# One beat less of lag in the gate pipeline of a transformer block, and its last copies shared by two engines

## The chip, the cores and the metric

The kernel runs on one core of a Trainium2 chip. The metric is the device time of one execution in microseconds (us). TensorE multiplies and transposes, ScalarE and VectorE work element by element, GpSimd does the same for work off their hands, and SyncE issues DMAs. Each engine runs its own queue in order; engines meet by semaphores only.

## The reference

The reference is a transformer block on x of 4 x 32 x 32 x 192: attention with decomposed relative positions (12 heads of 16), then a mixture of 8 experts in which each of the 4096 tokens takes its best one. The change touches what lies between the two:

```python
x = x + _L0_conv_ref(_ln_c(x), ...)          # ends with: out @ proj_w.T + proj_b
t = _to_tokens(x)
t = t + _L0_ffn_ref(_ln_t(t), ...)           # begins with: gate = xf @ Wg.T + bg
...
def _ln_t(v, eps=1e-05):
    m = jnp.mean(v, axis=-1, keepdims=True)
    s = jnp.var(v, axis=-1, keepdims=True)
    return (v - m) / jnp.sqrt(s + eps)
```

## The kernel before

Five functions run one after the other, with all engines meeting between them: `project`, `attention`, `gate` (L960), `route` (L1274) and `experts` (L1386). The change is in `gate` alone. It handles the 4096 tokens in 8 steps of 512 tokens (`STEPS`), each of 4 tiles of 128 tokens (`TPS`). What a step s goes through, with the short names that this document uses:

- **T(s), A(s)**: `turn_attention` (L1061) transposes the attention output on TensorE into `at_ps`; `copy_attention` (L1126) copies its two parts on ScalarE.
- **P(s)**: `project_out` (L1070), 16 float32 matmuls on TensorE. Its input is A(s).
- **R(s)**: `residual` (L1181) on VectorE, two additions into x_sb and four of statistics.
- **root**: `take_root` for the steps of `ROOTS`: (0, 1), (2, 3), (4, 5), (6) and (7), called roots 0 to 4. VectorE makes the variance in five small instructions (L1247 to L1253), ScalarE takes the square root (L1138), VectorE makes `rstd` and `shift` in five more (L1257 to L1265). In each engine's queue nothing passes it.
- **N(s)**: `normalize` (L1034) on GpSimd, four instructions (L1042), which need the root of the step. The last step's is on VectorE (L1219), after root 4.
- **H(s)**: `split_high` (L1148) on ScalarE, the float16 high part of the normalized rows (L1154).
- **L(s)**: `split_low` (L1192) on VectorE, the rest that H(s) leaves (L1195).
- **D(s)**: `double_tails` (L1045) on GpSimd (L1049); after it SyncE stores the step's parts to HBM (L1016), the residual having been stored at L1012.
- **U(s)**: `turn_normalized` (L1083) on TensorE, 8 transposes of the high half and 8 of the low half into two PSUM banks, one bank for each half (L1091).
- **C(s)**: `copy_normalized` (L1140) on ScalarE, the high and the low bank, 128x1024 float16 each (L1146).
- **G(s)**: `gates` (L1094) on TensorE, 16 small matmuls into `gate_ps`.

After G(7), VectorE adds the bias to the gate values (L1226, L1228), and the engines meet before `route` begins.

The order in each queue is written out by hand, as a loop over beats b. With `LAG = 3`, a beat of the kernel before is, for all b at which the step numbers are valid:

- TensorE: T(b+1), P(b), U(b-4), G(b-5)
- ScalarE: A(b+1), the square root of the root that ended at beat b-1, H(b-3), C(b-4)
- VectorE: L(b-4), R(b), the root that ends with step b; at b = 7 also L(4) and N(7); L(5) to L(7) after it
- GpSimd: D(b-4), N(b-2)
- SyncE: the residual's store of b, the parts' store of b-4

Waits that bear on the order: T(s) needs A(s-1); U(s) needs D(s) and both halves of C(s-1); G(s) needs C(s); C(s) needs U(s) and G(s-2); N(s) and H(s) need their slot of three free, that is L(s-3), and for H(s) also U(s-3) and the store of s-3.

Of the kernel before, what the change touches and what calls it, by code (L numbers as in the profile page):

```python
# [20 lines left out]
ALU = mybir.AluOpType  # L21
ACT = mybir.ActivationFunctionType
# [11 lines left out]
STEPS = T // HALF  # L34
TPS = HALF // P
# [924 lines left out]
def gate(nc, g):  # L960

    LAG = 3
    ROOTS = ((0, 2), (2, 4), (4, 6), (6, 7), (7, 8))
    BANKS, SLOTS = 3, 3
    CONSTS = 16 * (7 + len(ROUTE_TABLES))
# [2 lines left out]
    with ExitStack() as ctx:  # L968
        sb = lambda name, shape, dt=F32: ctx.enter_context(nc.sbuf_tensor(name, shape, dt))
        sem = lambda name: ctx.enter_context(nc.semaphore(name))  # L970
        w, wg = g.proj_w, g.gate_w
        at = [sb("at_top", [C, 2, HALF]), sb("at_bottom", [C + 1, 2, HALF])]
        tt = [sb("tt_hi", [P, 2, 2 * HALF], F16), sb("tt_lo", [P, 2, 2 * HALF], F16)]
# [17 lines left out]
        last_ready = sem("last_tn_ready")  # L991
        tn_hi_done, tn_lo_done, tails_doubled = sem("tn_hi_done"), sem("tn_lo_done"), sem("tails_doubled")
        x1_stored, tn_stored = sem("x1_stored"), [sem(f"tn_stored{j}") for j in range(SLOTS)]
        tt_ps_ready, tt_ready, gate_ready, gate_copied = sem("tt_ps_ready"), sem("tt_ready"), sem("gate_ready"), sem("gate_copied")
        gate_split = sem("gate_split")
        block = ctx.enter_context(nc.Block())

# [7 lines left out]
        @block.sync  # L1005
        def _(sp):
            load_experts(sp, g, experts_loaded)

            def store_residual(s):
                sp.wait_ge(x1_ready, 2 * s + 2)  # L1010
                tiles = slice(TPS * s, TPS * (s + 1))
                sp.dma_start(g.token_tiles[:, tiles, AT_X:ROW], g.x_sb[:, tiles, :]).then_inc(x1_stored, 16)  # L1012

            def store_normalized(s):
                sp.wait_ge(tails_doubled, s + 1)
                sp.dma_start(g.token_tiles[:, TPS * s:TPS * (s + 1), 0:AT_X],  # L1016
                             parts[:, s % SLOTS].rearrange("p t q d -> p t (q d)").bitcast(F32)).then_inc(tn_stored[s % SLOTS], 16)

            for b in range(STEPS + LAG + 1):
                if b < STEPS:  # L1020
                    store_residual(b)
                if b >= LAG + 1:
                    store_normalized(b - LAG - 1)
            sp.wait_ge(x1_stored, 16 * STEPS)
            for j in range(SLOTS):
                sp.wait_ge(tn_stored[j], 16 * len(range(j, STEPS, SLOTS)))
            sp.wait_ge(experts_loaded, 16 * (EXPERTS // 2))

        @block.gpsimd
        def _(pool):  # L1030
            nc.gpsimd.memset(g.slot_rows[:], 0.0).then_inc(rows_zeroed, 1)
            pool.wait_ge(rows_zeroed, 1)

            def normalize(s):  # L1034
                pool.wait_ge(shift_done, root_of(s) + 1)
                if s >= SLOTS:

                    pool.wait_ge(tn_hi_done, s - SLOTS + 1)
                    pool.wait_ge(tn_lo_done, s - SLOTS + 1)
                for i in range(TPS):  # L1040
                    t = TPS * s + i
                    last = nc.gpsimd.tensor_scalar(tn[:, s % SLOTS, i, :], g.x_sb[:, t, :], rstd[:, t:t + 1], shift[:, t:t + 1], ALU.mult, ALU.add)  # L1042
                last.then_inc(tn_ready, 1)

            def double_tails(s):  # L1045

                pool.wait_ge(tn_lo_done, s + 1)
                both = parts[:, s % SLOTS]
                nc.gpsimd.tensor_copy(both[:, :, :, D:ROW_PART], both[:, :, :, P:D]).then_inc(tails_doubled, 1)  # L1049

            for b in range(2, STEPS + LAG + 1):
                if b >= LAG + 1:
                    double_tails(b - LAG - 1)
                if b - 2 < STEPS - 1:
                    normalize(b - 2)

        @block.tensor
        def _(pe):
# [23 lines left out]

            def turn_normalized(s):  # L1083
                pe.wait_ge(tails_doubled, s + 1)
                if s:
                    pe.wait_ge(tt_ready, 2 * s)
                for part in range(2):
                    for i in range(TPS):
                        for c in range(2):
                            at = c * HALF + i * P  # L1090
                            last = nc.tensor.transpose(tt_ps[part][:, at:at + P], parts[:, s % SLOTS, i, part, c * P:(c + 1) * P], g.ident16[:])  # L1091
                    last.then_inc(tt_ps_ready, 1)

            def gates(s):  # L1094
                pe.wait_ge(tt_ready, 2 * s + 2)
                for i in range(TPS):
                    t = TPS * s + i
                    both, high = (g_ps[:, 2 * t * EXPERTS:(2 * t + n) * EXPERTS] for n in (2, 1))
                    (top_hi, tail_hi), (top_lo, tail_lo) = ([rows[:, s % 2, c * HALF + i * P:c * HALF + (i + 1) * P] for c in range(2)] for rows in tt)
                    nc.tensor.matmul(both, top_hi, w16[0][:], start=True, stop=False, skip_group_check=True)  # L1100
                    nc.tensor.matmul(high, top_lo, w16[0][:, 0:EXPERTS], start=False, stop=False, skip_group_check=True)
                    nc.tensor.matmul(high, tail_hi, w16[1][:, 0:EXPERTS], start=False, stop=False, skip_group_check=True)
                    last = nc.tensor.matmul(high, tail_lo, w16[1][:, EXPERTS:], start=False, stop=True, skip_group_check=True)
                last.then_inc(gate_ready, 1)

            turn_attention(0)
            pe.wait_ge(ones_set, 1)
            for b in range(STEPS + LAG + 2):
                if b + 1 < STEPS:
                    turn_attention(b + 1)  # L1110
                if b < STEPS:
                    project_out(b)
                if LAG + 1 <= b < STEPS + LAG + 1:
                    turn_normalized(b - LAG - 1)
                if b == LAG + 2:
                    pe.wait_ge(gate_split, 6)
                if b >= LAG + 2:
                    gates(b - LAG - 2)

        @block.scalar  # L1120
        def _(act):
# [15 lines left out]
                tiles = slice(TPS * first, TPS * last)  # L1137
                nc.scalar.activation(rstd[:, tiles], var[:, tiles], ACT.Sqrt).then_inc(root_done, 1)  # L1138

            def copy_normalized(s):  # L1140
                for c in range(2):
                    act.wait_ge(tt_ps_ready, 2 * s + c + 1)
                    if s >= 2 and c == 0:

                        act.wait_ge(gate_ready, s - 1)
                    nc.scalar.activation(tt[c][:, s % 2, :], tt_ps[c][:], ACT.Copy).then_inc(tt_ready, 1)  # L1146

            def split_high(s):  # L1148
                wait_normalized(act, s)
                if s >= SLOTS:  # L1150

                    act.wait_ge(tn_stored[s % SLOTS], 16 * (s // SLOTS))
                    act.wait_ge(tt_ps_ready, 2 * (s - SLOTS) + 2)
                nc.scalar.activation(parts[:, s % SLOTS, :, 0, 0:D], tn[:, s % SLOTS], ACT.Copy).then_inc(tn_hi_done, 1)  # L1154

            copy_attention(0)
            for b in range(STEPS + LAG + 1):
                if b + 1 < STEPS:
                    copy_attention(b + 1)
                if b - 1 in ended:  # L1160
                    take_root(ended[b - 1])
                if LAG <= b < STEPS + LAG:
                    split_high(b - LAG)
                if b >= LAG + 1:
                    copy_normalized(b - LAG - 1)

        @block.vector
        def _(dve):
# [23 lines left out]
            def split_low(s):  # L1192
                dve.wait_ge(tn_hi_done, s + 1)
                both = parts[:, s % SLOTS]
                nc.vector.tensor_tensor(both[:, :, 1, 0:D], tn[:, s % SLOTS], both[:, :, 0, 0:D], ALU.subtract).then_inc(tn_lo_done, 1)  # L1195
# [4 lines left out]
                inverse_root(nc, dve, stats, mean, var, rstd, shift, tmp, EPS_FFN, chain, root, root_done, shift_done,  # L1200
                             tiles=slice(TPS * first, TPS * last), calls=r)

            for b in range(STEPS + LAG + 1):
                if LAG + 1 <= b < STEPS:
                    split_low(b - LAG - 1)
                if b < STEPS:
                    residual(b)
                if b in ended:
                    take_root(ended[b])
                if b == STEPS - 1:  # L1210

                    split_low(b - LAG)
                    s = STEPS - 1
                    dve.wait_ge(shift_done, len(ROOTS))
                    dve.wait_ge(tn_hi_done, s - SLOTS + 1)
                    dve.wait_ge(tn_lo_done, s - SLOTS + 1)
                    for i in range(TPS):
                        t = TPS * s + i
                        nc.vector.tensor_scalar(tn[:, s % SLOTS, i, :], g.x_sb[:, t, :], rstd[:, t:t + 1], shift[:, t:t + 1],  # L1219
                                                ALU.mult, ALU.add).then_inc(last_ready, 1)  # L1220
                if b > STEPS:
                    split_low(b - LAG - 1)
# [485 lines left out]
```

## Time and profile before

| | us |
|---|---|
| median of 3 runs | 914.4 (911.68 to 914.62) |
| the profiled execution's own time | 910.65 |
| its span, first to last instruction | 908.8 |
| `project` | 0 to about 85 |
| `attention` | to about 672 |
| `gate` | about 672 to 731 |
| `route` | about 731 to 752 |
| `experts` | to the end |

Over the whole span TensorE is busy 89%, VectorE 80%, ScalarE 67% and GpSimd 30%. These shares say little on the change, since it lies in 59 of 909 us: in there, what counts is which wait ends last before each engine's next instruction. Times of the trace are counted from the start of the span.

### The profile page before, as it was taken

What the parts mean: (1) busy time and instruction counts of PE and PEld (TensorE: products, weight loads), DVE (VectorE), ACT (ScalarE), POOL (GpSimd) and SP (SyncE); (2) the same over time, 40 slices, a digit from 0 to 9 for tenths busy, and PEclk for the clock granted to TensorE, in tenths of its full rate; (3) what the DMA queues carried; (4) which work ended last, traced back from release to release, by engine and by line L of the source; (5) the groups of instructions that cost most, each with busy time, mean ns of one, the idle gap of its engine ahead of it and who ended that gap; (6) DMA issues with size and microseconds to landing.
All of it is one profiled execution on the core that took longest, in us unless ns stands there. A gap on an engine that the chain in (4) does not pass through costs nothing. (4 is left out here: it accounts for less than half of the span.)

```text
span 908.8 us, 26203 instructions
## 1 busy us (share of the span) xinstructions
PE 810.6 (89%) x8970; PEld 448.2 (49%) x8970; DVE 725.3 (80%) x1026; ACT 611.1 (67%) x1139; POOL 275.9 (30%) x431
## 2 busy tenths in 40 slices
PE   3889946999999999999999999999989526999994
PEld 1657931333333333333333333333348516999994
DVE  6756766898899989999999999989627676888883
ACT  3556623888888888888888888888865513444452
POOL 2460000013342343302223242431114404656552
PEclk9989975999999999999999999999999757999998
DMA  6234783344544444434444444553135402222320
GB/s 170 79 91 130 321 313 91 96 119 132 141 133 120 135 131 129 118 113 122 131 134 131 138 132 120 140 152 98 25 122 169 159 16 70 80 83 80 88 60 12
DMA packets 69733, 109.63 MB, mean 121 GB/s; under 512 B 20139, under 2 KB 36681, under 8 KB 68146
## 3 DMA queue, kind: packets, MB, share of 16 engines
q1 hardware_dynamic: 59120, 75.49, 28.6%
q0 software_dynamic: 9248, 26.51, 10.0%
q10 hardware_dynamic: 1314, 6.95, 2.0%
q8 instruction: 31, 0.51, 0.2%
q14 instruction: 20, 0.16, 0.1%
HBM read 77.58 MB, written 33.19 MB: 122 GB/s over the span
## 5 line engine op out<-in xcount | busy, mean ns | idle before, releaser
L907 DVE TENSOR_REDUCE neg_max<-max_ps 128x1 f16<-128x1024 f32 x384 | 452.2, 1222 | 54.4 <-PE max_ps L761 54.0
L890 ACT ACTIVATE probs<-ring_ps 128x512 f32<-128x512 f32 x768 | 413.6, 595 | 69.9 <-PE ring_ps L793 68.5
L793 PE MATMUL ring_ps<-q_side,k_side 113*128 113x512 f16 x768 | 234.6, 387 | 6.0 <-DMA q_side<-rel_split 4.0
L805 PE MATMUL out_ps<-probs,values 128*32 128x256 f32 x3072 | 206.4, 386 | 0.1
L761 PE MATMUL max_ps<-k_side,q_side 48*128 48x256 f16 x1536 | 123.0, 279 | 15.6 <-ACT ident L865 9.1
L805 PEld LDWEIGHTS out_ps<-probs,values 128*32 128x32 f32 x3072 | 80.3, 109 | 111.1 <-ACT probs L890 56.2
L657 POOL COPY max_copies<-neg_max 128x32 f16<-128x32 f16 x48 | 10.1, 211 | 365.7 <-DVE neg_max L907 365.7
L761 PEld LDWEIGHTS max_ps<-k_side,q_side 48*128 48x128 f16 x1536 | 50.2, 95 | 114.6 <-issue 66.4
L793 PEld LDWEIGHTS ring_ps<-q_side,k_side 113*128 113x128 f16 x768 | 51.8, 97 | 104.9 <-ACT probs L890 73.1
L1461 PE MATMUL hid_ps<-slot_t,w_top 128*118 128x128 f16 x312 | 69.6, 223 | 0.8 <-ACT slot_t L1507 0.8
L1462 PE MATMUL hid_ps<-slot_t,w_top 128*118 128x128 f16 x312 | 68.9, 221 | 0.0
L1463 PE MATMUL hid_ps<-slot_t,w_top 128*118 128x128 f16 x312 | 68.9, 221 | 0.0
L1464 PE MATMUL hid_ps<-slot_t,w_tail 128*118 128x128 f16 x312 | 68.9, 221 | 0.0
L1465 PE MATMUL hid_ps<-slot_t,w_tail 128*118 128x128 f16 x312 | 68.9, 221 | 0.0
L1517 ACT ACTIVATE silu<-hid_ps 118x512 f32<-118x512 f32 x39 | 23.3, 597 | 50.5 <-PE hid_ps L1465 50.5
L1440 POOL DMA_INDIRECT out<-y,slot_token x39 | 39.5, 1012 | 54.4 <-issue 36.8
L1425 POOL DMA_INDIRECT slot_rows<-token_rows,slot_token x39 | 42.2, 1082 | 39.1 <-SPq L1388 27.4
L1564 DVE TENSOR_TENSOR hidden<-hid_ps,silu 118x512 f32<-118x512 f32 x39 | 27.0, 691 | 27.2 <-ACT silu L1517 19.4
L1461 PEld LDWEIGHTS hid_ps<-slot_t,w_top 128*118 128x118 f16 x312 | 41.9, 134 | 4.0 <-issue 2.3
L1462 PEld LDWEIGHTS hid_ps<-slot_t,w_top 128*118 128x118 f16 x312 | 42.0, 135 | 0.0
L1463 PEld LDWEIGHTS hid_ps<-slot_t,w_top 128*118 128x118 f16 x312 | 42.0, 135 | 0.0
L1465 PEld LDWEIGHTS hid_ps<-slot_t,w_tail 128*118 128x118 f16 x312 | 42.0, 134 | 0.0
(228 smaller groups left out, 1321.0 us busy)
## 6 DMA issues: line engine op xcount, KB each, us to landing
q_side<-rel_split SPq DMA_DIRECT2D x384, 64.0 KB, 2.3
q_side<-qk_split SPq DMA_DIRECT2D x192, 64.0 KB, 2.5
rel_split<-expert_weights ACTq DMA_DIRECT2D x6, 1024.0 KB, 5.0
rel_split<-expert_weights SPq DMA_DIRECT2D x6, 1024.0 KB, 6.1
q_side<-qk_split SPq DMA_DIRECT2D x48, 128.0 KB, 2.7
k_side<-qk_split SPq DMA_DIRECT2D x144, 32.0 KB, 1.7
token_rows<-tn_parts SPq DMA_DIRECT2D x8, 512.0 KB, 3.5
expert_weights<-in_w_t POOLq DMA_DIRECT2D x32, 117.2 KB, 2.9
```

The costliest lines, as they stand in the source:

```text
L761: last = nc.tensor.matmul(max_ps[t % 2][:, keys], q_side[j][at:at + HIGH, quarter, t * P:(t + 1) * P], k_side[j][at:at + HIGH, keys], star ...
L793: nc.tensor.matmul(ring_ps[turn_of(k) % BANKS][:], k_side[slot(s)][:, tile * P:(tile + 1) * P], q_side[slot(s)][:, tile // 2, (i % 2) * HA ...
L805: last = nc.tensor.matmul(out_ps[quarter * 2 * HD:(quarter + 1) * 2 * HD, :], values[j][:, tile, :], probs[:, u % 2 * GROUP + 2 * i + quar ...
L890: nc.scalar.activation(probs[:, u % 2 * GROUP + i, :], ring_ps[turn_of(k) % BANKS][:], ACT.Exp).then_inc(exp_done, 1)
L907: nc.vector.tensor_reduce(neg_max[:, j % 2, t:t + 1], max_ps[t % 2][:], AX, ALU.max, negate=True).then_inc(tile_max, 1)
L1425: pool.indirect_dma_start(rows[:, j, :], None, g.token_rows, bass.IndirectOffsetOnAxis(ap=g.slot_token[:, n:n + 1], axis=0), bounds_check= ...
L1440: pool.indirect_dma_start(g.out_rows, bass.IndirectOffsetOnAxis(ap=g.slot_token[:, n:n + 1], axis=0), y[:, j, :], None, bounds_check=last_ ...
L1461: nc.tensor.matmul(out, w_top[:, j, h, 0, some], hi_top, start=True, stop=False, skip_group_check=True)
L1462: nc.tensor.matmul(out, w_top[:, j, h, 0, some], lo_top, start=False, stop=False, skip_group_check=True)
L1463: nc.tensor.matmul(out, w_top[:, j, h, 1, some], hi_top, start=False, stop=False, skip_group_check=True)
L1464: nc.tensor.matmul(out, w_tail[:, j, h, some], hi_tail, start=False, stop=False, skip_group_check=True)
L1465: last = nc.tensor.matmul(out, w_tail[:, j, h, some], lo_tail, start=False, stop=True, skip_group_check=True)
```

## The change

Every later member of a step's chain moves up by one beat, relative to T(b+1), P(b) and R(b), which stay. A beat is now:

- TensorE: T(b+1), P(b), U(b-3), G(b-4)
- ScalarE: A(b+1), the square root, H(b-2), C(b-3). After beat 7: root 4, H(6), high half of C(5), H(7), high half of C(6), high half of C(7)
- VectorE: L(b-3), R(b), the root. After beat 7: L(5), N(7), L(6), L(7), low halves of C(5), C(6), C(7)
- GpSimd: D(b-3), N(b-2); at b = 7 N(5) and N(6) both
- SyncE: the residual's store of b, the parts' store of b-3

The semaphore `tt_ready` becomes two, one for each half, so that U(s) can begin with the high half when the high bank is free. The number of instructions that compute is the same; three copies move from ScalarE to VectorE.

```diff
+    EARLY = STEPS - LAG
...
-            for b in range(2, STEPS + LAG + 1):
-                if b >= LAG + 1:
-                    double_tails(b - LAG - 1)
-                if b - 2 < STEPS - 1:
+            for b in range(2, STEPS + LAG):
+                if b >= LAG:
+                    double_tails(b - LAG)
+                if b < STEPS:
                     normalize(b - 2)
+                if b == STEPS - 1:
+                    normalize(STEPS - 2)
...
                 pe.wait_ge(tails_doubled, s + 1)
-                if s:
-                    pe.wait_ge(tt_ready, 2 * s)
                 for part in range(2):
+                    if s:
+                        pe.wait_ge(tt_ready[part], s)
...
-                if LAG + 1 <= b < STEPS + LAG + 1:
-                    turn_normalized(b - LAG - 1)
+                if LAG <= b < STEPS + LAG:
+                    turn_normalized(b - LAG)
...
             copy_attention(0)
-            for b in range(STEPS + LAG + 1):
+            for b in range(STEPS):
                 if b + 1 < STEPS:
                     copy_attention(b + 1)
                 if b - 1 in ended:
                     take_root(ended[b - 1])
-                if LAG <= b < STEPS + LAG:
-                    split_high(b - LAG)
-                if b >= LAG + 1:
-                    copy_normalized(b - LAG - 1)
+                if b >= 2:
+                    split_high(b - 2)
+                if b >= LAG:
+                    for c in range(2):
+                        copy_turned(b - LAG, c)
+            take_root(len(ROOTS) - 1)
+            split_high(STEPS - 2)
+            copy_turned(STEPS - 3, 0)
+            split_high(STEPS - 1)
+            copy_turned(STEPS - 2, 0)
+            copy_turned(STEPS - 1, 0)
...
+            def copy_low(s):
+                dve.wait_ge(tt_ps_ready, 2 * s + 2)
+                dve.wait_ge(gate_ready, s - 1)
+                nc.vector.tensor_copy(tt[1][:, s % 2, :], tt_ps[1][:]).then_inc(tt_ready[1], 1)
+
+            for b in range(STEPS):
+                if b >= LAG:
+                    split_low(b - LAG)
+                residual(b)
                 if b in ended:
                     take_root(ended[b])
...
+            for n in range(EARLY + 1, STEPS):
+                split_low(n)
+            for n in range(EARLY, STEPS):
+                copy_low(n)
```

## Rows read from the trace of the kernel before

**Rows 1.** Stretches: length, busy per engine (instructions), TensorE clock, DMA share, GB/s.
```profile
693.00:715.00 22.00, 15.40 (x179) 14.37 (x177) 16.81 (x62) 13.21 (x20) 10.89 (x20) 0.98 0.50 164
715.00:731.00 16.00, 9.72 (x144) 9.35 (x144) 6.38 (x11) 9.22 (x10) 5.24 (x8) 0.50 0.40 138
```

**Rows 2.** Waits of 672 to 731: who, for whom, us in total, times, longest.
```profile
POOL tn_parts L1049 <- DVE tn_parts L1195: 18.6, 6, 5.0
ACT tt_hi L1146 <- PE tt_hi_ps L1091: 14.0, 8, 3.0
DVE rstd L1257 <- ACT rstd L1138: 3.2, 5, 1.2
```

**Rows 3.** Timeline of VectorE, L(3) and L(4): start, duration, instruction, idle before.
```profile
708.84 0.18 DVE L1257 RECIPROCAL rstd<-rstd 128x4 f32<-128x4 f32 x1 [0.68 <-ACT rstd L1138]
...
709.72 0.95 DVE L1195 TENSOR_TENSOR tn_parts<-tn,tn_parts 128x768 f16<-128x768 f32 x1
...
715.07 0.95 DVE L1195 TENSOR_TENSOR tn_parts<-tn,tn_parts 128x768 f16<-128x768 f32 x1
```

**Rows 4.** Timeline of GpSimd, of the same beats.
```profile
710.73 0.61 POOL L1049 COPY tn_parts<-tn_parts 128x512 f16<-128x512 f16 x1 [2.78 <-DVE tn_parts L1195]
711.32 1.98 POOL L1042 TENSOR_SCALAR tn<-x_sb,rstd,shift 128x192 f32<-128x192 f32 x4
```

**Rows 5.** Timeline of ScalarE, beats 5 to 7.
```profile
702.17 0.59 ACT L1132 ACTIVATE at_top<-at_ps 96x512 f32<-96x512 f32 x1
...
703.12 0.22 ACT L1138 ACTIVATE rstd<-var 128x8 f32<-128x8 f32 x1
...
706.70 1.02 ACT L1146 ACTIVATE tt_hi<-tt_hi_ps 128x1024 f16<-128x1024 f16 x1 [2.63 <-PE tt_hi_ps L1091]
707.62 1.02 ACT L1146 ACTIVATE tt_lo<-tt_lo_ps 128x1024 f16<-128x1024 f16 x1
708.53 0.21 ACT L1138 ACTIVATE rstd<-var 128x4 f32<-128x4 f32 x1
```

**Rows 6.** Timeline of ScalarE: the first H, and the end of `gate`.
```profile
688.89 0.84 ACT L1154 ACTIVATE tn_parts<-tn 128x768 f16<-128x768 f32 x1 [0.90 <-POOL tn L1042]
...
728.40 1.02 ACT L1146 ACTIVATE tt_lo<-tt_lo_ps 128x1024 f16<-128x1024 f16 x1
```

**Rows 7.** Timeline of VectorE: N(7) and the gate values.
```profile
716.16 1.74 DVE L1219 TENSOR_SCALAR tn<-x_sb,rstd,shift 128x192 f32<-128x192 f32 x4
...
730.10 0.42 DVE L1226 TENSOR_TENSOR gates_sb<-gate_ps,gate_bias 128x256 f32<-128x256 f32 x1 [5.22 <-PE gate_ps L1103]
```

**Rows 8.** Timeline of TensorE: T(4) and T(5) at full clock, U and G at half.
```profile
686.28 1.04 PE L1067 MATMUL at_ps<-ident_sb,att_sb 128*96 128x128 f32 x8
...
689.77 1.04 PE L1067 MATMUL at_ps<-ident_sb,att_sb 128*96 128x128 f32 x8
...
717.58 1.06 PE L1091 MATMUL tt_lo_ps<-ident,tn_parts 128*128 128x128 f16 x8
718.43 0.22 PE L1100 MATMUL gate_ps<-gate_top_parts,tt_hi 128*128 128x16 f16 x1
```

**Rows 9.** Groups of VectorE instructions near to a copy out of PSUM.
```profile
L907 DVE TENSOR_REDUCE neg_max<-max_ps 128x1 f16<-128x1024 f32 x384 | 452.2, 1222 | 54.4 <-PE max_ps L761 54.0
L1545 DVE COPY w<-w_all 128x1536 f16 x39 | 21.2, 545 | 0.0
L1343 DVE COPY total<-count_ps 128x256 f32<-128x256 f32 x1 | 0.4, 425 | 0.8 <-PE count_ps L1306 0.8
```

**Rows 10.** Stretches where TensorE's clock falls and rises (columns as in rows 1).
```profile
712.80:716.75 3.95, 0.05 (x2) 0.00 (x1) 2.92 (x13) 2.02 (x4) 1.17 (x3) 0.64 0.65 211
...
757.00:758.00 1.00, 0.22 (x3) 0.18 (x3) 0.00 (x0) 0.87 (x2) 0.69 (x2) 0.50 0.37 135
...
761.00:762.00 1.00, 1.00 (x14) 1.00 (x13) 0.00 (x0) 0.33 (x1) 0.16 (x1) 0.64 0.47 151
```

**Rows 11.** SyncE's stores of the parts (L1016): issue to landing, min/median/max.
```profile
DMA to landing us min/median/max: 2.9/3.5/4.9
```

More of the change, by code:

```diff
@@ L993, in gate @@
         x1_stored, tn_stored = sem("x1_stored"), [sem(f"tn_stored{j}") for j in range(SLOTS)]
-        tt_ps_ready, tt_ready, gate_ready, gate_copied = sem("tt_ps_ready"), sem("tt_ready"), sem("gate_ready"), sem("gate_copied")
+        tt_ps_ready, tt_ready, gate_ready, gate_copied = sem("tt_ps_ready"), [sem("tt_hi_ready"), sem("tt_lo_ready")], sem("gate_ready"), sem("gate_copied")
         gate_split = sem("gate_split")
@@ L1017, in store_normalized @@
                              parts[:, s % SLOTS].rearrange("p t q d -> p t (q d)").bitcast(F32)).then_inc(tn_stored[s % SLOTS], 16)
-            for b in range(STEPS + LAG + 1):
+            for b in range(STEPS + LAG):
                 if b < STEPS:
                     store_residual(b)
-                if b >= LAG + 1:
-                    store_normalized(b - LAG - 1)
+                if b >= LAG:
+                    store_normalized(b - LAG)
             sp.wait_ge(x1_stored, 16 * STEPS)
@@ L1094, in gates @@
             def gates(s):
-                pe.wait_ge(tt_ready, 2 * s + 2)
+                for part in range(2):
+                    pe.wait_ge(tt_ready[part], s + 1)
                 for i in range(TPS):
@@ L1107, in _ @@
             pe.wait_ge(ones_set, 1)
-            for b in range(STEPS + LAG + 2):
+            for b in range(STEPS + LAG + 1):
                 if b + 1 < STEPS:
@@ L1112, in _ @@
                     project_out(b)
-                if LAG + 1 <= b < STEPS + LAG + 1:
-                    turn_normalized(b - LAG - 1)
-                if b == LAG + 2:
+                if LAG <= b < STEPS + LAG:
+                    turn_normalized(b - LAG)
+                if b == LAG + 1:
                     pe.wait_ge(gate_split, 6)
-                if b >= LAG + 2:
-                    gates(b - LAG - 2)
+                if b >= LAG + 1:
+                    gates(b - LAG - 1)
         @block.scalar
@@ L1138, in take_root, with copy_turned @@
                 nc.scalar.activation(rstd[:, tiles], var[:, tiles], ACT.Sqrt).then_inc(root_done, 1)
[L1140 to L1146, printed above, removed]
+            def copy_turned(s, c):
+                act.wait_ge(tt_ps_ready, 2 * s + c + 1)
+                if s >= 2:
+                    act.wait_ge(gate_ready, s - 1)
+                nc.scalar.activation(tt[c][:, s % 2, :], tt_ps[c][:], ACT.Copy).then_inc(tt_ready[c], 1)
             def split_high(s):
@@ L1156, in _ @@
             copy_attention(0)
-            for b in range(STEPS + LAG + 1):
+            for b in range(STEPS):
                 if b + 1 < STEPS:
@@ L1161, in _ @@
                     take_root(ended[b - 1])
-                if LAG <= b < STEPS + LAG:
-                    split_high(b - LAG)
-                if b >= LAG + 1:
-                    copy_normalized(b - LAG - 1)
+                if b >= 2:
[9 more added lines that the diff above has]
+            copy_turned(STEPS - 1, 0)
         @block.vector
@@ L1201, in take_root @@
                              tiles=slice(TPS * first, TPS * last), calls=r)
[L1203 to L1207, printed above, removed]
+            def copy_low(s):
[3 more added lines that the diff above has]
+            for b in range(STEPS):
+                if b >= LAG:
+                    split_low(b - LAG)
+                residual(b)
                 if b in ended:
                     take_root(ended[b])
[L1210 to L1222, printed above, removed]
+            split_low(EARLY)
+            s = STEPS - 1
+            dve.wait_ge(shift_done, len(ROOTS))
+            dve.wait_ge(tn_hi_done, s - SLOTS + 1)
+            dve.wait_ge(tn_lo_done, s - SLOTS + 1)
+            for i in range(TPS):
+                t = TPS * s + i
+                nc.vector.tensor_scalar(tn[:, s % SLOTS, i, :], g.x_sb[:, t, :], rstd[:, t:t + 1], shift[:, t:t + 1],
+                                        ALU.mult, ALU.add).then_inc(last_ready, 1)
+            for n in range(EARLY + 1, STEPS):
+                split_low(n)
+            for n in range(EARLY, STEPS):
+                copy_low(n)
             dve.wait_ge(gate_ready, STEPS)
```

## The prediction

> **What bounds the kernel now.** The change lies in `gate`, 59 of 909 us, so I read first what each engine does in that stretch. From 693 to 715 no engine is full: VectorE, the busiest, works 16.81 of 22.00 us [rows 1]. A stage in which nobody is full is set by a loop of waits, and the table of waits gives its shape: GpSimd waits 18.6 us for L, ScalarE 14.0 us for U [rows 2]. The timelines give the order. From L(3) to L(4) it is 715.07 - 709.72 = 5.35 us [rows 3]. The loop closes through a queue, not through data: L(b-4), D, U, the two copies C(b-4) on ScalarE, and behind them in ScalarE's queue the square root of beat b, for which VectorE waits with everything that follows, the next L first [rows 3, 5]. H(b-3) and N(b-2) are not on this loop: N starts when D has been done [rows 4], and has a whole beat before H asks for it.
>
> The end is another chain: from L(4), right behind the last root at 715.07, to the gate values at 730.10, 15.03 us [rows 3, 7]. Everything after `gate` waits for these values, so what `gate` gains or loses is the kernel's.
>
> **What the change does to the loop.** Now H(b-2) stands ahead of C(b-3) on ScalarE. H(b-2) needs N(b-2); N(b-2) stands behind D(b-3) on GpSimd; D(b-3) needs L(b-3). So N and H, which lay beside the loop, are in it. What is queued behind H's wait: both copies, A and the square root; and VectorE waits for that root with L, R and the next root. Step by step, start to start:
>
> - L to D: 710.73 - 709.72 = 1.01 us [rows 3, 4]
> - D to N 0.59, N 1.98 [rows 4], and 0.03 to the next engine: 2.60
> - H until ScalarE's next instruction: 0.84 less the 0.1 by which neighbours overlap there, 0.75 [rows 5, 6]
> - C, high and low: 0.92 + 0.91 = 1.83 us [rows 5]
> - A, where there is one: 703.12 - 702.17 = 0.95 us [rows 5]
> - square root to reciprocal 0.31, reciprocal to the next L 0.88 [rows 3, 5]
>
> The sum is 7.38 us, with A 8.33, in place of 5.35. U, P and R are no longer on it: U(b-3) needs D alone and is done while N and H run; R comes before the root, and the root's first half is over some 3 us before the square root is given.
>
> Laid out from the first H, at 688.89 as before, since nothing ahead of it is moved [rows 6]: L(0) at 689.76 (it now stands ahead of R(3) and waits 1 us there, which P(3) covers), N(1) 691.4, H(1) 693.4, C(0), A(5), L(1) 8.33 after L(0), at 698.09. Beat 4 has no root, so L(2) follows when H(2) is done, after 1.01 + 2.60 + 0.86 = 4.47 us: 702.56. Then L(3) 8.33 later, 710.89; L(4) 718.27; L(5), behind root 4, 725.65. In the kernel before the instruction behind root 4 started at 715.07. **The last root comes 10.58 us later.** Of this 3.2 us are there by L(4); the rest is that root 4 now stands one whole loop of 7.38 us behind L(4), since its square root stands behind H(5) and C(4).
>
> The stores move up by a beat with D. H(5) to H(7) need the stores of 2 to 4. The closest is H(7), at 729.3, with the store of 4 issued about 720; landing takes 2.9 to 4.9 us [rows 11], so it is hidden. So is the last store: issued at about 732, landed by 735.5, at the slowest 736.9, against a meeting of the engines at about 737.3.
>
> **What it does to the end.** From L(5) at 725.65:
>
> - VectorE: N(7) 726.5, 1.74 us at most [rows 7], L(6) by 728.3. Nobody waits for them last
> - D(5) 726.66, U(5) high 727.33. TensorE has the half clock here, as before [rows 1]: 8 transposes take 1.06, and the next instruction begins 0.85 after their start [rows 8]
> - C(5) high 728.4, H(7) 729.3 to 730.15, L(7) 730.2, 0.87 until the next
> - low half of C(5) on VectorE 731.05 for q us, behind L(7) in its queue
> - U(6) low begins when that is done, then G(5), U(7) high, U(7) low, with low C(6) beside them; then low C(7) of q us, G(7), and the gate values 0.68 us after the last copy, as before (728.40 + 1.02 to 730.10) [rows 6, 7]
>
> With q = 0.68: U(6) low 731.8, G(5) 732.6, U(7) high 733.1, U(7) low 734.0, low C(7) 735.1 to 735.75, **gate values 736.4**. The change is 736.4 - 730.1 = **+6.3 us**: 10.58 later, with an end of 10.8 in place of 15.0 us.
>
> **The price q** has no row: VectorE copies no 1024 float16 out of PSUM. Its reduction reads 1024 elements of PSUM in 1.22 us; its copy of 256 float32 from there takes 0.425; 1536 float16 from SBUF take 0.545 [rows 9]. The line through the two PSUM rows is 0.16 fixed and 1.06 for 1024 elements; the SBUF copy shows that float16 goes through at more than two in that time. I take two: 0.16 + 0.53, about 0.68, between the ends of 0.42 and 1.22. At q = 1.22 two of the copies are in the chain in full and one in part: +7.6. At q = 0.42 C(7) high on ScalarE gets nearly as late: +5.8. Below nothing it can't go, since C(7) high alone still ends at about 735.
>
> The Trainium skill, VectorE: DVE Perf Modes, section "Why PSUM operands drop a tier", allows a 16-bit copy out of PSUM two elements a cycle at the most, and its section on the TRN2 errata gives 120 + FD/Accel cycles at 0.96 GHz: an estimate of 0.66 us. By it the sum would be +6.3; no run here shows it so far.
>
> The split of `tt_ready` saves nothing in the loop, as D comes after C there; in the end it lets U(6) high go 0.9 us before its low half, which is not last.
>
> **Against the measure.** The profiled execution took 910.65, its span 908.8 and 1.85 around it; it would be 917.0. The median of the three runs, 914.4, lies 3.75 above it. The prediction is made against the median: 914.4 + 6.3 = 920.7.
>
> **The rivals.**
>
> 1. *Faster: N and H stay beside the loop.* The loop keeps its 5.35 us, the last root its place, and the shorter end is all: -4.2, 910.2. It decides at one point: H(b-2) would have to start by the end of D(b-3), when U(b-3) starts, to be over when U's high half is. For it speaks that GpSimd waits 18.6 us in all [rows 2], long enough for N. Against it: D(b-3) stands ahead of N(b-2) in the queue, in every beat from 3, so N can't use that time. Chance 0.06.
> 2. *Slower still: the clock halves inside the projection.* U(0) starts at about 691.4 and T(5) and P(4) follow for 3.49 us [rows 8]; from 695.8 to U(1) at 699.8 TensorE would stand idle. An idle of 3.95 us brought the clock to 0.50, a mean of 0.64 over it; work resumed before 758, and it came back between 761 and 762 [rows 10]. If it returns so quickly here, P(5) ends at about 706.3 instead of 704.6, and R(5) is still in time. But if it stays at half through P(7), T and P take 7.0 us instead of 3.49, P(5) to P(7) end at 709.0, 718.2 and 725.6, the U behind each of them late, and the last root comes 4.0 us later again: +10.3, 924.7. The Trainium skill, TensorE: Matmul & The Clock Gate, section "Part 4: PE-mode transpose", says that transposes do not count as work that frees the clock, and U(1) and T(6) are 24 transposes in a row but for 16 small matmuls; by it the return is later. No row here tells them apart. Chance 0.12.
> 3. *Same: part of it is made up.* The end would have to gain 4 us more (low copies at nothing, U at full clock), or `route` to have slack to the gate values. The former ends at C(7) high, as said; against the latter stands that VectorE waits 5.2 us for these values [rows 7]. 914.4. Chance 0.07.
>
> My forecast has the rest, 0.75, with its own range of 919 to 923.
>
> **How the numbers follow.** A measurement of this kernel can tell about 0.3%, 2.7 us. Faster by more: rival 1, 0.06. Within: rival 3 and the forecast's edge, 0.08. Slower by more: the forecast and rival 2, 0.86. The range starts at 910.65 + 5.8, less half a microsecond for what adds up over so many steps, 916.0, as single runs of the kernel lie between 910.65 and 914.62; it reaches up over rival 2 to 925.5.
>
> **What would show it.** In the profile after: L to L 7.4 to 8.3 us in beats with a root, 4.5 in the one without; H waiting for N in each beat, and C no longer for U; VectorE's wait for the square root up from 3.2 us in all [rows 2] to about 12; the step behind root 4 at 725.6; gate values at 736.4; low copies of 0.68 us. It is wrong if N starts before its D, if L to L stays near 5.4, or if the clock is at 0.5 from 697 on.

## The result and the profile after

The changed kernel takes 920.93 us (median of 17 runs, 915.25 to 923.71) against 912.16 (17 runs, 909.08 to 916.41). The ratio is 1.0086, 95% interval 1.0068 to 1.0103: 7.8 us slower, between 6.2 and 9.4. The profiled executions are 917.31 and 910.65, their spans 915.5 and 908.8.

All of it lies in `gate`. In both traces `gate` is entered at about the same time (the first N starts at 686.52, before at 686.91), and from the gate values to the end of the span it is 178.69 us after and 178.70 before. Between first H and gate values it is 48.31 against 41.21: +7.10 us. The interval of the ratio holds these 7.1 us. One execution of e12_pe_busy_14 below took 986.24 us at a granted clock of 0.82, in a slower state of the chip, and is not in that kernel's ratio.

The stretches of the changed kernel, which answer [rows 1] (length, busy of TensorE, of its weight loads, VectorE, ScalarE, GpSimd with their instructions, TensorE's clock, DMA share, GB/s):

```profile
693.00:715.00 22.00, 16.80 (x164) 16.08 (x164) 12.14 (x42) 11.36 (x18) 7.65 (x15) 0.84 0.39 129
715.00:731.00 16.00, 8.45 (x85) 7.77 (x84) 9.17 (x30) 7.84 (x11) 5.81 (x11) 0.61 0.39 133
```

VectorE works 12.14 of 22.00 us where it worked 16.81: less gets done in the same stretch. The waits of 672 to 738 say for whom, and answer [rows 2]:

```profile
POOL tn_parts L1050 <- DVE tn_parts L1205: 27.1, 8, 6.4
ACT tn_parts L1157 <- POOL tn L1043: 20.7, 6, 4.6
DVE rstd L1271 <- ACT rstd L1142: 10.2, 5, 3.6
ACT tt_hi L1149 <- PE tt_hi_ps L1094: 6.6, 4, 3.1
```

The second line is new in kind: H (L1157) waits 20.7 us for N, where it waited 0.9. C's wait for U has fallen from 14.0 to 6.6, of which 6.1 come after root 4, and VectorE's wait for the square root has risen from 3.2 to 10.2. One turn of the loop, from L(3) to L(4), in the timelines of VectorE, GpSimd and ScalarE (start, duration, instruction, idle before):

```profile
711.21 0.95 DVE L1205 TENSOR_TENSOR tn_parts<-tn,tn_parts 128x768 f16<-128x768 f32 x1
...
717.69 0.18 DVE L1271 RECIPROCAL rstd<-rstd 128x4 f32<-128x4 f32 x1 [2.69 <-ACT rstd L1142]
...
718.57 0.95 DVE L1205 TENSOR_TENSOR tn_parts<-tn,tn_parts 128x768 f16<-128x768 f32 x1
```
```profile
712.23 0.61 POOL L1050 COPY tn_parts<-tn_parts 128x512 f16<-128x512 f16 x1 [6.44 <-DVE tn_parts L1205]
712.82 1.98 POOL L1043 TENSOR_SCALAR tn<-x_sb,rstd,shift 128x192 f32<-128x192 f32 x4
```
```profile
714.83 0.84 ACT L1157 ACTIVATE tn_parts<-tn 128x768 f16<-128x768 f32 x1 [4.64 <-POOL tn L1043]
715.58 1.00 ACT L1149 ACTIVATE tt_hi<-tt_hi_ps 128x1024 f16<-128x1024 f16 x1
716.48 1.01 ACT L1149 ACTIVATE tt_lo<-tt_lo_ps 128x1024 f16<-128x1024 f16 x1
717.39 0.20 ACT L1142 ACTIVATE rstd<-var 128x4 f32<-128x4 f32 x1
```

Read them as one chain: L(3) 711.21, D(3) 712.23, N(4) 712.82, H(4) 714.83 after 4.64 us of waiting, the two copies 715.58 and 716.48, the square root 717.39, the reciprocal 717.69, L(4) 718.57. That is 7.36 us, where [rows 3] have 5.35. In this turn the copies wait for nobody; they only stand in the way of the square root.

The end, in VectorE's timeline, answering [rows 6, 7]:

```profile
725.94 0.95 DVE L1205 TENSOR_TENSOR tn_parts<-tn,tn_parts 128x768 f16<-128x768 f32 x1
...
735.39 0.69 DVE L1216 COPY tt_lo<-tt_lo_ps 128x1024 f16<-128x1024 f16 x1 [1.44 <-PE tt_lo_ps L1094]
736.81 0.42 DVE L1240 TENSOR_TENSOR gates_sb<-gate_ps,gate_bias 128x256 f32<-128x256 f32 x1 [0.72 <-PE gate_ps L1107]
```

From the instruction behind root 4 (L(5), 725.94) to the gate values it is 10.87 us in place of 15.03, and the low copy takes 0.69 us.

### The profile page after: what moved, and what is told of

It is laid out like the page before. It is cut to its first block and busy times, and to the rows that moved or that the text cites. A ratio compares the mean times of both kernels' runs of the same rounds, so it can differ in the third digit from the quotient of the medians.

```text
span 915.5 us, 26216 instructions
## 1 busy us (share of the span) xinstructions
PE 813.5 (89%) x8970; PEld 451.2 (49%) x8970; DVE 728.8 (80%) x1029; ACT 607.9 (66%) x1136; POOL 273.8 (30%) x431
## 3 DMA queue, kind: packets, MB, share of 16 engines
q0 software_dynamic: 9248, 26.51, 10.2%
## 5 line engine op out<-in xcount | busy, mean ns | idle before, releaser
L1475 PEld LDWEIGHTS hid_ps<-slot_t,w_top 128*118 128x118 f16 x312 | 42.0, 135 | 3.6 <-issue 1.7
L1476 PEld LDWEIGHTS hid_ps<-slot_t,w_top 128*118 128x118 f16 x312 | 42.2, 135 | 0.0
L1479 PEld LDWEIGHTS hid_ps<-slot_t,w_tail 128*118 128x118 f16 x312 | 42.1, 135 | 0.0
L1478 PEld LDWEIGHTS hid_ps<-slot_t,w_tail 128*118 128x118 f16 x312 | 42.1, 135 | 0.0
```

The costliest lines, as they stand in the source:

```text
L1475: nc.tensor.matmul(out, w_top[:, j, h, 0, some], hi_top, start=True, stop=False, skip_group_check=True)
L1476: nc.tensor.matmul(out, w_top[:, j, h, 0, some], lo_top, start=False, stop=False, skip_group_check=True)
L1478: nc.tensor.matmul(out, w_tail[:, j, h, some], hi_tail, start=False, stop=False, skip_group_check=True)
L1479: last = nc.tensor.matmul(out, w_tail[:, j, h, some], lo_tail, start=False, stop=True, skip_group_check=True)
```

## The experiments

Two marks are read from each trace: X, from the first H to the instruction behind root 4 on VectorE (L(4) with the old lag, L(5) with the shorter one), and Y, from there to the gate values. X and Y are of one execution each, and TensorE's clock alone can move them by a microsecond or two (e4_end_only below); the ratio is of many executions, to the kernel before on the same chip. Whole spans of single traces are not compared: behind the gate values, where the code is the same, they hold between 175.7 and 179.6 us.

| kernel | X | Y | X + Y | against before | ratio, 95% interval |
|---|---|---|---|---|---|
| before | 26.18 | 15.03 | 41.21 | | |
| changed | 37.44 | 10.87 | 48.31 | +7.10 | 1.0086, 1.0068 to 1.0103 |
| e1_n_first | 35.05 | 10.90 | 45.95 | +4.74 | 1.0038, 1.0014 to 1.0062 |
| e2_c_first | 33.65 | 10.86 | 44.51 | +3.30 | 1.0021, 0.9999 to 1.0043 |
| e7_root_first | 28.23 | 10.86 | 39.09 | -2.12 | 0.9953, 0.9930 to 0.9976 |
| e4_end_only | 27.82 | 13.34 | 41.16 | -0.05 | 0.9969, 0.9940 to 0.9999 |
| e5_before_n_twice | 28.24 | 15.04 | 43.28 | +2.07 | 1.0011, 0.9991 to 1.0032 |
| e6_after_n_twice | 46.56 | 9.73 | 56.29 | +15.08 | 1.0170, 1.0132 to 1.0207 |
| e3_loop_only | 36.84 | 10.57 | 47.41 | +6.20 | 1.0068, 1.0041 to 1.0096 |
| e8_pe_busy | 37.86 | 10.88 | 48.74 | +7.53 | 1.0097, 1.0065 to 1.0129 |
| e12_pe_busy_14 | 36.76 | 10.89 | 47.65 | +6.44 | 1.0068, 1.0043 to 1.0094 |
| e9_root_ahead_of_h | 27.15 | 9.72 | 36.87 | -4.34 | 0.9955, 0.9931 to 0.9978 |
| e10_and_last_h_first | 27.15 | 10.38 | 37.53 | -3.68 | 0.9944, 0.9921 to 0.9968 |
| e11_old_lag_root_ahead | see below | 15.03 | | +0.50 | 0.9989, 0.9966 to 1.0013 |

The theory to be tested (theory 1): the beat became longer since N and H came into the loop that closes through the square root. Its rivals are TensorE's half clock (theory 2) and the stores (theory 3).

### Is N in the loop? N doubled, in both kernels

```diff
+                    if 1 <= s <= 5:
+                        nc.gpsimd.tensor_scalar(spare[:, TPS * (s - 1) + i, :], g.x_sb[:, t, :], rstd[:, t:t + 1], shift[:, t:t + 1], ALU.mult, ALU.add)
                     last = nc.gpsimd.tensor_scalar(tn[:, s % SLOTS, i, :], ...)
```

> The changed kernel with the same doubling of N(1) to N(5). Theory 1 (N is in the loop in every beat): 1.98 us more in each of five beats, L to L of 9.3 us in steps 3 and 4, X from 37.4 to about 47.3, Y as it is: some 9.9 us more than the changed kernel. If N were beside the loop, as in the kernel before, it would be 1.5 to 2.5 us.

> The kernel before with each of the 20 instructions of N(1) to N(5) issued a second time into a spare tile, so N takes 3.96 us in place of 1.98 in five steps; what is computed stays the same. Theory 1 (N lies beside the loop in the kernel before): the L to L of 5.35 us stay in steps 3 and 4, and only N(2), with D(1) behind it, is late once: X from 26.2 to about 27.7, Y as before, 1.5 us in all and at most 2.5. Theory 2 or 3: no word on N.

On the changed kernel L to L rose to 10.34, 6.42, 10.31, 9.31 and 9.31 us, from 8.39, 4.46, 8.99, 7.36 and 7.37: 1.95 more in four of the five beats, which is N's own 1.98, and 1.3 in the third, where a late TensorE had cost something already. X is up 9.12 where 9.9 were expected, the ratio 1.0170 in four executions. Y is 1.1 us shorter than in the changed kernel, with TensorE's clock at 0.95 from 740.0 to 745.5. H's wait for N, in the table of waits of 672 to 747, is now the longest of the stage:

```profile
ACT tn_parts L1160 <- POOL tn L1046: 30.5, 6, 6.6
```

On the kernel before the same 9.9 us of added GpSimd work cost 2.06 us at X (1.5 were expected) and nothing that the runs can tell (1.0011, 0.9991 to 1.0032). N lies beside the loop there, in it here. That is the theory's main claim, and neither rival has a word for it. L(3) to L(4) did grow there too, from 5.35 to 5.82, which was not expected; this is told under the hardware.

### The order of the queues, one at a time

The changed kernel with one line moved each time. First GpSimd, N ahead of D:

```diff
-                if b >= LAG:
-                    double_tails(b - LAG)
                 if b < STEPS:
                     normalize(b - 2)
+                if b >= LAG:
+                    double_tails(b - LAG)
```

> The changed kernel with N(b-2) ahead of D(b-3) in GpSimd's queue, nothing else. Two marks are used for all runs: X, from the first H to the instruction behind root 4 on VectorE (before 26.2 us, changed kernel 37.4), and Y, from there to the gate values (15.0 and 10.9). Theory 1 (N and H have come into the loop because N stands behind D on GpSimd and C, A and the square root behind H on ScalarE): N(3) and N(5), whose root is long there, now run early; N(2) and N(4) still wait for their root and hold D. X about 30.0, Y 10.9, so about 7 us less than the changed kernel and within 1 us of the kernel before. Theory 2 (TensorE's half clock in the projection makes P and U late): N's place is of no matter, X stays at 37. Theory 3 (the stores, issued a beat earlier beside other traffic, hold H): X stays at 37.

X fell by 2.4 us where 7.4 were expected. The direction fits theory 1 and neither of the others, the size was a miss. L to L is 7.12, 3.68, 10.67, 7.36 and 5.35. The last beat did what was said: N(5) had its root long before, and the loop fell from 7.37 to 5.35. But from L(3) to L(4) nothing was won: N(4) comes out of root 2 just then, now D(3) waits behind N(4), U(3) behind D(3), and C(3) behind U(3). The wait moved from one member of the loop to another. And the third beat took 10.67 us: R(5) waited 3.92 us for P(5), which stands behind U(1) and T(6) on TensorE. The half clock is about 1.4 us of this: T(6) and P(5) took 4.88 us, from 699.79 to 704.67, in place of 3.49, with 0.66 as the mean clock from 698 to 703.

Second ScalarE, the copies ahead of H:

```diff
                     take_root(ended[b - 1])
-                if b >= 2:
-                    split_high(b - 2)
                 if b >= LAG:
                     for c in range(2):
                         copy_turned(b - LAG, c)
+                if b >= 2:
+                    split_high(b - 2)
```

> The changed kernel with C(b-3) ahead of H(b-2) in ScalarE's queue, nothing else. Theory 1: N runs beside U and C, and the loop is L, D, U, C, H, square root: 1.01 + 0.65 + 0.65 + 1.83 + 0.75 + 0.31 + 0.88 = 6.1 us in place of 7.4; X about 32.2, Y 10.9, some 4.5 to 5 us less than the changed kernel, and about 2 us more than the kernel before. Theory 2 (half clock): C waits for U in either order, X stays at 37 or grows. Theory 3 (stores): no change, as H waits as long.

L(4) to L(5) is 6.08 us, as worked out (6.1), and L(3) to L(4) 6.45; X is 33.65, 3.8 less than the changed kernel, where 5.2 were expected; the rest went in the second to the fourth beat (5.46, 7.69 and 6.45), with U(1) at the half clock and a mean of 0.64 from 699 to 702.

Third the square root, taken in the beat of its root, ahead of the copies:

```diff
-                if b - 1 in ended:
-                    take_root(ended[b - 1])
                 if b >= 2:
                     split_high(b - 2)
+                if b in ended:
+                    take_root(ended[b])
                 if b >= LAG:
...
-            take_root(len(ROOTS) - 1)
```

> The changed kernel with each square root taken in the beat of its root, behind H(b-2) and ahead of C(b-3), in place of the beat after. Theory 1: both copies and A leave the loop: L, D, N, H, square root, 1.01 + 2.60 + 0.85 + 0.31 + 0.88 = 5.65 us; X about 28, Y 10.9: some 9 us less than the changed kernel and 2.4 us less than the kernel before, 0.3%. Theory 2: X stays above 35. Theory 3: H waits as long as now, X stays above 35.

X is 28.23 and Y 10.86, as expected to 0.3 us. In ScalarE's timeline the square root of root 3 now stands ahead of the copies:

```profile
710.98 0.19 ACT L1142 ACTIVATE rstd<-var 128x4 f32<-128x4 f32 x1
711.07 1.00 ACT L1149 ACTIVATE tt_hi<-tt_hi_ps 128x1024 f16<-128x1024 f16 x1
```

The copies and A are out of the loop, L to L is 5.61, 4.48, 5.86, 5.54 and 5.86, and the kernel is faster than the one before: 2.1 us in the profiles, 4.3 (2.2 to 6.4) by the ratio of 0.9953. What made the change slow was not the shorter lag, but the square root's place behind the work that the shorter lag had put ahead of it.

### The end and the loop apart

> The changed kernel with its beats, but all copies C on ScalarE to the end. Theory 1: X stays at 37.4, since the loop isn't touched, and Y is about 11.7 in place of 10.9, since H(7) waits for the low copy of C(5) and the last two copies lie one behind the other: 0.8 us more than the changed kernel. That would give the change's parts: the moved steps +11.3 at X and most of the -4.1 at Y, the shared copies only 0.8 of it.

```diff
             split_high(STEPS - 2)
-            copy_turned(STEPS - 3, 0)
+            for c in range(2):
+                copy_turned(STEPS - 3, c)
             split_high(STEPS - 1)
-            copy_turned(STEPS - 2, 0)
-            copy_turned(STEPS - 1, 0)
+            for s in range(STEPS - 2, STEPS):
+                for c in range(2):
+                    copy_turned(s, c)
...
-            for n in range(EARLY, STEPS):
-                copy_low(n)
```

With the copies back on ScalarE the loss stays (1.0068), so it is the loop's. Y was expected at 11.7 and came out at 10.57, less than with shared copies. In this execution TensorE's clock came back to 1.00 between 730 and 731, and the last 16 transposes went at twice the pace; in the changed kernel's it was at half until all the transposes were done. What the shared copies are worth here is not shown by this run: the two ratios overlap.

> The kernel before, its beats and lag unchanged, with the changed kernel's end: tt_ready in two halves, high copies of steps 4 to 7 on ScalarE and low copies on VectorE, H(6) and H(7) ahead of the high copy of C(5). Theory 1: X stays at 26.2, Y falls from 15.0 to about 12.7, where TensorE at the half clock (U and G, 2.1 us a step) sets it: about 2.3 us less than the kernel before, ratio 0.9975. If sharing the copies brings nothing, Y stays at 15 and the ratio at 1.000.

```diff
...
+            take_root(len(ROOTS) - 1)
+            split_high(STEPS - 3)
+            copy_turned(STEPS - 4, 0)
+            split_high(STEPS - 2)
+            split_high(STEPS - 1)
+            copy_turned(STEPS - 3, 0)
+            copy_turned(STEPS - 2, 0)
+            copy_turned(STEPS - 1, 0)
...
+            split_low(STEPS - 3)
+            copy_low(STEPS - 4)
+            split_low(STEPS - 2)
+            split_low(STEPS - 1)
+            for n in range(STEPS - 3, STEPS):
+                copy_low(n)
```

The end of its own is worth something, 0.9969, though the interval reaches to 0.9999. Y fell by 1.7 us, not 2.3. X should have been 26.2 and is 27.8, in a loop whose code is that of the kernel before, and so X + Y shows no gain in this trace: the clock fell after P(4) here, 0.87 from 696 to 699 and 0.56 to 702, where it was 1.00 in the trace of before, and P(5) with R(5) came late.

### The half clock by itself

In the changed kernel TensorE stood idle between P(4) and U(1), and the clock fell in it (stretches as above):

```profile
695.60:699.40 3.80, 0.01 (x1) 0.00 (x0) 2.43 (x8) 1.14 (x4) 0.62 (x2) 0.78 0.02 4
699.40:703.00 3.60, 3.56 (x39) 3.50 (x40) 2.07 (x6) 1.65 (x3) 1.91 (x4) 0.50 0.67 224
703.00:704.60 1.60, 1.60 (x8) 1.59 (x7) 0.18 (x1) 1.60 (x4) 1.35 (x3) 0.51 0.21 70
704.60:712.00 7.40, 6.92 (x69) 6.55 (x68) 4.41 (x17) 4.21 (x7) 1.18 (x3) 1.00 0.38 125
```

It stayed at 0.50 over U(1), T(6) and the beginning of P(5). To see what that costs, matmuls that nobody reads fill the gap:

```diff
+                if b == LAG + 1:
+                    pe.wait_ge(x1_ready, 2 * b)
+                    for _ in range(30):
+                        nc.tensor.matmul(p_ps[1][:, HALF - P:HALF], g.ident[:], g.ident[:], start=True, stop=True, skip_group_check=True)
```

> The changed kernel with 30 float32 matmuls of 128 columns, which nobody reads, on TensorE behind P(4), in the 3.8 us in which it stood idle before U(1) and after which the clock was at half. Theory 1, with the half clock as a small second term: the clock stays at 1.00 to U(1), P(5) ends at full rate, C(2) no longer waits for U(2), the L to L from L(2) to L(3) falls from 9.0 to 8.35 us, X from 37.4 to 36.8. Theory 2 (the half clock is what makes the kernel slower): X falls to 30 or less.

Too many: they took 6.86 us and ran past D(1), so U(1) began 2.8 us behind the end of D(1) and X did not fall (37.86). But the clock was at 1.00 from 688 to 710, and the kernel was as slow as ever: the half clock isn't what made it slow. With 14 instead of 30, and its stretches below:

> The changed kernel with 14 float32 matmuls behind P(4) in place of 30, which had run on past D(1) and kept U(1) waiting. 14 take about 3.2 us, and end before D(1). The clock stays at 1.00 to U(1), P(5) ends at full rate, the L to L from L(2) to L(3) is 8.35 us in place of 9.0, X 36.8 in place of 37.4. Theory 2 (the half clock is what costs the most): X falls to 30 or less.

```profile
695.80:699.80 4.00, 3.32 (x30) 3.13 (x28) 2.45 (x8) 1.31 (x4) 0.65 (x2) 1.00 0.02 3
699.80:705.00 5.20, 5.18 (x63) 5.12 (x64) 2.91 (x8) 3.27 (x5) 3.27 (x7) 1.00 0.52 176
```

The stretches show the clock at 1.00 over the filled gap and over U(1) to P(5). L(2) to L(3) is 8.34 us (8.99 in the changed kernel, 8.35 expected), X 36.76 (36.8 expected). So by the traces the half clock costs about 0.7 us of the 7.1; the other 6.4 are what the longer loop costs (10.6 us more at X) less what the shorter end gives back (4.1 at Y). The two ratios, 1.0068 and 1.0086, can't be told apart. e3_loop_only shows the same with no edit: there the clock fell later, and L(2) to L(3) is 8.36.

### A version that is faster than both

> The changed kernel with each square root in its own beat and ahead of H(b-2), in place of behind H(b-2). Theory 1: now N and H leave the loop too, and what is left is VectorE's own work between two L: L 0.87, R 2.09, the root's two halves and the square root, 5.0 us, some 5.3 where GpSimd's N slows the root's small instructions as it did with N doubled. X about 26 (28.2 with the root behind H), Y 10.9: gate values about 2 us earlier, some 6 us less than the kernel before in the runs of this chip, ratio about 0.993 to 0.996. If the loop isn't closed through the square root, X stays at 28.

```diff
-                if b - 1 in ended:
-                    take_root(ended[b - 1])
+                if b in ended:
+                    take_root(ended[b])
                 if b >= 2:
                     split_high(b - 2)
...
-            take_root(len(ROOTS) - 1)
```

L(3) to L(4) is 5.02 us and VectorE waits 1.7 us in all for the five square roots; ScalarE now waits for VectorE, 13.1 us (its table of waits, 672 to 731):

```profile
ACT rstd L1142 <- DVE var L1266: 13.1, 5, 4.4
...
DVE rstd L1270 <- ACT rstd L1142: 1.7, 5, 0.3
```

X is 27.15, a microsecond above what was expected: two beats took 5.88 and 5.83. In the first R(5) waits for P(5); the second is told under the hardware. The ratio is 0.9955.

> As the run before it, and in the end H(7) ahead of the high copy of C(5) on ScalarE. H(7)'s input is ready 0.5 us before that copy's. L(7) and with it the low copies on VectorE begin 1.3 us earlier, the high copy of C(5) 0.3 us later: Y about 9.9 in place of 10.9, X as in the run before it: 1 us less again. If the end is set by TensorE's half clock alone, Y stays at 10.9.

Against e9_root_ahead_of_h:

```diff
-            copy_turned(STEPS - 3, 0)
             split_high(STEPS - 1)
+            copy_turned(STEPS - 3, 0)
```

Y is 10.38, 0.5 less than the 10.86 to 10.90 of the kernels with the changed kernel's end at the half clock, half of what was expected. Against e9_root_ahead_of_h Y can't be read, since there the clock came back before the end and Y was 9.72. The ratio is 0.9944, 0.9921 to 0.9968. The two kernels can't be told apart; either is about 0.5% faster than the kernel before, where the changed one is 0.9% slower.

> The kernel before, its lag and its end unchanged, with each square root in its own beat, ahead of H(b-3) and C(b-4). Theory 1: the copies leave the loop, which falls from 5.35 to VectorE's own 5.0: X about 24.6 in place of 26.2, Y 15.0: 1.6 us less than the kernel before. It tells what the square root's place is worth without the change, and so what a beat less of lag is worth once the place is mended: Y 10.9 against 15.0, X 26 against 24.6, 2.7 us for the shorter lag.

```diff
-                if b - 1 in ended:
-                    take_root(ended[b - 1])
+                if b in ended:
+                    take_root(ended[b])
                 if LAG <= b < STEPS + LAG:
                     split_high(b - LAG)
```

The loop did fall, to 5.02 and 5.01 us in the last two beats. But nothing was gained, 0.9989, 0.9966 to 1.0013. At the old lag root 1's square root stands ahead of the first H, and holds it (timeline of ScalarE):

```profile
695.45 0.21 ACT L1138 ACTIVATE rstd<-var 128x8 f32<-128x8 f32 x1 [4.38 <-DVE var L1253]
695.57 0.83 ACT L1154 ACTIVATE tn_parts<-tn 128x768 f16<-128x768 f32 x1
```

H(0) came 5.98 us after the start of N(0), in place of 1.98, and X, which counts from it, says nothing here; from the start of N(0) to the gate values it is 43.69 us, before 43.19. About 0.8 us of it go with the clock, which fell here after P(4) (L(1) to L(2) took 8.69 us in place of 7.89). With the shorter lag, the shared end and the root in the same place (e9) it is 38.85. Part of these 4.8 us is the clock too, which came back early in e9; the medians on this chip, 912.04 and 907.91, lie 4.1 us apart. So the moved square root alone is worth nothing that the runs can tell, and the shorter lag with the shared end, on top of it, about 4 us, where 1.6 and 2.7 were expected. How those 4 us divide between the lag and the end isn't shown: the old lag with both the moved square root and the shared end was not run, and the shared end alone has 0.9969 (e4_end_only), whose interval overlaps those of e9 and e10.

## Why the prediction was right, and where it was off

**The bound.** The loop through the square root and the chain of the end were what the trace of before showed. The kernels with one line moved confirm the loop; e4_end_only and e10_and_last_h_first, whose end was changed and whose Y moved, speak for the end.

**The loop.** 7.38 us were worked out without A and 7.36 and 7.37 measured; with A 8.33 against 8.39 for the first; in the beat without a root 4.47 against 4.46. Every duration came from the trace of before, and those in the loop came out within 0.03 us, since the instructions stayed the same and only their order moved.

**The third beat.** Here a step failed, that of rival 2: "If it returns so quickly here, P(5) ends at about 706.3 instead of 704.6, and R(5) is still in time." P(5) ended at 706.55. This trace runs 0.39 us ahead of the layout (first H at 688.50, not 688.89), so it was 0.64 us later than said: the half clock lasted longer. R(5) was in time all the same. But U(2) stands behind P(5) in TensorE's queue, and C(2) behind U(2). The trace after has them so, in TensorE's and in ScalarE's timeline:

```profile
706.55 0.61 PE L1094 MATMUL tt_hi_ps<-ident,tn_parts 128*128 128x128 f16 x8
```
```profile
707.20 1.02 ACT L1149 ACTIVATE tt_hi<-tt_hi_ps 128x1024 f16<-128x1024 f16 x1 [0.54 <-PE tt_hi_ps L1094]
```

C(2) begins 0.54 us after it could have. I had followed the late P(5) to the one that reads its result and not to what is queued behind it. It is most of what is missing: X was 36.76 by the layout, 37.44 in the trace, and 36.76 with the clock kept (e12_pe_busy_14).

**The end.** 10.8 against 10.87 us. The low copy was taken at 0.68 us from three rows of other instructions and took 0.69. The Trainium skill, VectorE: DVE Perf Modes, section "Why PSUM operands drop a tier", with its section on the TRN2 errata, gave an estimate of 0.66; the trace agrees to 0.03 us, and with two elements a cycle out of PSUM.

**What else was said.** Full slowing at the half clock (rival 2 in its dear form) did not come: the clock was back at 704.6. VectorE's wait for the square root was to be about 12 us and was 10.2, for the late third beat shortened one of the waits. The stores held nobody: in no trace does H wait for one. Rival 1 fell as it was argued, with D ahead of N, but e1_n_first shows that the argument was too simple: moving N ahead frees only those beats in which N's root is old.

**The sum.** +7.10 in the traces for +6.3, and +7.8 (6.2 to 9.4) by the runs. That the median of 920.93 lies so close to the 920.7 is luck: the base was 914.4 from 3 runs and is 912.16 from 17, 2.2 us too high, and the medians lie 8.8 us apart, 2.5 more than was said. The two errors cancel.

## What to carry to other kernels

In a pipeline written out by hand over in-order queues, shortening the lag can put a wait for a slow neighbour ahead of work that others need. Before doing it, write down the loop that closes through the queues, member by member, and ask of each small instruction on which another engine waits (here a 0.2 us square root) what stands ahead of it. In the changed kernel moving that one line was worth 9.2 us (e7_root_first) and 11.4 us (e9_root_ahead_of_h) in the traces, more than the change had cost; in the kernel before (e11_old_lag_root_ahead) it was worth nothing that the runs can tell. When an engine is late, follow what is queued behind it as well as who reads its result.

## What the runs showed of the hardware

**GpSimd and VectorE slow each other.** In the kernel before with N doubled, N ran beside the second half of the roots, and two of VectorE's smallest instructions took over twice their time (timeline of VectorE, root 3):

```profile
706.29 0.18 DVE L1260 RECIPROCAL rstd<-rstd 128x4 f32<-128x4 f32 x1 [0.40 <-ACT rstd L1141]
706.50 0.37 DVE L1262 TENSOR_TENSOR tmp<-rstd 128x4 f32<-128x4 f32 x1
706.91 0.43 DVE L1264 SCALAR_TENSOR_TENSOR tmp<-tmp,var 128x4 f32<-128x4 f32 x1
707.37 0.16 DVE L1266 SCALAR_TENSOR_TENSOR rstd<-tmp,rstd 128x4 f32<-128x4 f32 x1
```

GpSimd's instructions of 0.50 us stood beside them. Undisturbed each takes 0.16. The two long ones ended at 706.87 and 707.34, where a GpSimd instruction ended too (706.35 and 706.83, each with 0.50): the trace looks as if they had waited it out. It is why L to L grew from 5.35 to 5.82 there, and why the last beat of e9_root_ahead_of_h, with N(5) and N(6) beside root 4, took 5.83 instead of 5.02. The Trainium skill, SBUF — State Buffer, section "Who interferes with whom", says that a VectorE instruction with two SBUF inputs contends with a GpSimd instruction that reads SBUF; the trace agrees, with 0.43 us for 0.16.

It goes the other way as well. In the same trace L(1) began at 693.20 and took 1.03 us, and the GpSimd instruction that began 0.20 us later took 1.20 us in place of 0.50:

```profile
693.40 1.20 POOL L1045 TENSOR_SCALAR tn<-x_sb,rstd,shift 128x192 f32<-128x192 f32 x1
```

**The same queue and the same idle time give either clock.** After P(4) TensorE stood idle for 1.88 us in the kernel before and in e4_end_only alike. In the one trace the clock stayed at 1.00, in the other it fell to half (699 to 702 in the kernel before, then in e4_end_only):

```profile
699.00:702.00 3.00, 3.00 (x47) 2.93 (x46) 2.18 (x10) 2.25 (x3) 1.38 (x3) 1.00 0.28 91
```
```profile
699.00:702.00 3.00, 3.00 (x15) 2.91 (x14) 0.72 (x1) 2.87 (x5) 3.00 (x5) 0.56 0.80 264
```

From L(1) to L(2) it took 9.56 us in e4_end_only in place of 7.89. A profile of one execution shows one of the two.

**The clock came back over transposes.** In the end of e9_root_ahead_of_h TensorE did U(5), G(4) and the high half of U(6) at the half clock from 716.92 on, and was at 1.00 when the low half began at 721.40 (its stretches):

```profile
716.00:721.00 5.00, 3.27 (x40) 2.98 (x40) 3.65 (x8) 3.45 (x5) 1.50 (x3) 0.55 0.49 171
721.00:725.00 4.00, 2.95 (x72) 2.69 (x72) 1.84 (x4) 1.27 (x2) 0.41 (x1) 1.00 0.54 184
```

The Trainium skill, TensorE: Matmul & The Clock Gate, section "Part 4: PE-mode transpose", says that transposes don't count as work towards the full clock. The 40 instructions of the first row are 24 transposes and 16 matmuls of 8 or 16 columns, some 3.3 us of work of which the matmuls have about 0.5, and the clock returned; here the measurement speaks against the rule in its plain form. Whether the small matmuls brought the clock back, no run shows.
